# One core, macaron block in split fp32: turning two token units behind the first half of the first product

## What is computed

```python
x = x + 0.5 * ffn(layernorm(x))      # ffn: (silu(x @ Wg.T) * (x @ Wu.T)) @ Wd.T, hidden 2048
x = x + attn(layernorm(x))           # z = x @ W.T, four gated scans over time, layernorm, gamma, beta
x = x + 0.5 * ffn(layernorm(x))
```

## Time and profile before

| what | value |
|---|---|
| median of 3 runs | 1022.0 us (1021.89 to 1022.03) |
| the profiled execution, its own time | 1021.91 us |
| its span | 1020.1 us |
| TensorE matmul busy | 1014.9 us, 99% |
| VectorE, ScalarE, GpSimd busy | 671.1, 406.4, 162.1 us |
| granted TensorE clock, mean | 1.000 |

### The profile page before, as it was taken

The page is one execution under the profiler, slowest core; times in us unless marked ns, Lnnn a source line. Parts: engine busy times, 40 slices in busy tenths (PEclk is TensorE's granted clock), DMA queues, the critical chain, the costliest instruction groups (busy, mean ns, idle before and its releaser), DMA issues.

```text
span 1020.1 us, 12555 instructions
## 1 busy us (share of the span) xinstructions
PE 1014.9 (99%) x4512; PEld 841.5 (82%) x4512; DVE 671.1 (66%) x1013; ACT 406.4 (40%) x667; POOL 162.1 (16%) x187
## 2 busy tenths in 40 slices
PE   9999999999999999999999999999999999999998
PEld 8888888888888888888888888888888888888887
DVE  7755665598988687857978878786685333333342
ACT  6644445465433622224732363231382322222311
POOL 4123343125300200210430020021040000000000
PEclk9999999999999999999999999999999999999999
DMA  6688877778667555647856764454677565655255
GB/s 206 229 321 320 302 265 253 247 231 275 237 227 232 181 189 159 199 144 237 272 167 229 234 218 150 146 186 143 226 251 226 206 191 193 204 196 189 88 191 182
DMA packets 61710, 217.89 MB, mean 214 GB/s; under 512 B 6352, under 2 KB 15568, under 8 KB 53968
## 3 DMA queue, kind: packets, MB, share of 16 engines
q1 hardware_dynamic: 61072, 216.03, 63.1%
q10 hardware_dynamic: 576, 1.05, 0.3%
HBM read 170.92 MB, written 46.14 MB: 213 GB/s over the span
## 4 chain that ended last, share of the span: by engine, by line
PE 99%; DVE 1%; DMA 0%; DVEq 0%; issue 0%
PE ps_a L1538 8%; PE ps_a L1540 8%; PE ps_a L1539 8%; PE ps_b L1538 8%; PE ps_b L1540 8%; PE ps_b L1539 8%; PE ps_c L1538 7%; PE ps_c L1540 7%; PE ps_c L1539 7%; PE ps_d L1538 7%; PE ps_d L1540 7%; PE ps_d L1539 7%; PE aux L1539 3%; PE aux L1538 3%; PE aux L1540 3%; PE ps_d L1700 1%
## 5 line engine op out<-in xcount | busy, mean ns | idle before, releaser
L1035 DVE TENSOR_TENSOR tmp<-tmp,ps_c 128x512 f32<-128x512 f32 x59 | 40.4, 685 | 139.5 <-PE ps_c L1540 139.5
L1538 PE MATMUL ps_a<-xt,gu 128*128 128x512 f32 x304 | 118.3, 389 | 0.0
L1540 PE MATMUL ps_a<-xt,gu 128*128 128x512 f32 x304 | 118.3, 389 | 0.0
L1539 PE MATMUL ps_a<-xt,gu 128*128 128x512 f32 x304 | 118.3, 389 | 0.0
L1539 PE MATMUL ps_b<-xt,gu 128*128 128x512 f32 x286 | 111.3, 389 | 0.0
L1540 PE MATMUL ps_b<-xt,gu 128*128 128x512 f32 x286 | 111.3, 389 | 0.0
L1538 PE MATMUL ps_b<-xt,gu 128*128 128x512 f32 x286 | 111.3, 389 | 0.0
L1540 PE MATMUL ps_d<-dn,hid 128*128 128x512 f32 x256 | 99.6, 389 | 0.0
L1538 PE MATMUL ps_d<-dn,hid 128*128 128x512 f32 x256 | 99.6, 389 | 0.0
L1539 PE MATMUL ps_d<-dn,hid 128*128 128x512 f32 x256 | 99.6, 389 | 0.0
L1540 PE MATMUL ps_c<-xt,gu 128*128 128x512 f32 x236 | 91.8, 389 | 0.0
(11 more groups left out here) (204 smaller groups left out, 2111.5 us busy)
## 6 DMA issues: line engine op xcount, KB each, us to landing
dn<-dn_kept SPq DMA_DIRECT2D x112, 512.0 KB, 3.7
gu<-gu_kept SPq DMA_DIRECT2D x46, 1024.0 KB, 5.0
gu<-gu_kept SPq DMA_DIRECT2D x46, 768.0 KB, 5.6
gu_kept<-gu SPq DMA_DIRECT2D x14, 1024.0 KB, 4.3
gu_kept<-gu SPq DMA_DIRECT2D x14, 768.0 KB, 4.2
dn_kept<-dn SPq DMA_DIRECT2D x16, 512.0 KB, 5.1
h_t<-w_ffn_in SPq DMA_DIRECT2D x18, 256.0 KB, 4.8
x_tok<-w_ffn_in SPq DMA_DIRECT2D x18, 256.0 KB, 5.1
```

Source lines behind the costliest of these rows:

```text
L1035: dve.tensor_tensor(dst, u3s(si), p5_bank(si)[:, :], ALU.add).then_inc(c22_done, 1)
L1538: pe.matmul(dst, a_hi, b_hi, start=start, stop=False, skip_group_check=chained)
L1539: pe.matmul(dst, a_hi, b_lo, start=False, stop=False, skip_group_check=chained)
L1540: return pe.matmul(dst, a_lo, b_hi, start=False, stop=stop, skip_group_check=chained)
```

## The change

TensorE turns units 0 and 1 before the first product, as before. Units 2 and 3 are turned inside the first product, behind the first eight matmuls of the half that needs units 0 and 1 alone (high by high, low weights by high x). The filling matmuls stay behind unit 1. Nothing else is edited; the other engines' orders are the same.

```diff
@@ plain_first @@
                     if h == 0:
                         pe.wait_ge(raw_lo, 1)
                     plain_part(ps_a, 0, 0, 0, 1, 0, c)
+                    if h == 0:
+                        turn_x(2)
+                        turn_x(3)
                 for h, c in enumerate(halves):
                     pe.wait_ge(first_lo, 2 * h + 2)
@@ order of TensorE @@
             keep_warm(WARM)
-            for r in range(4):
+            for r in range(2):
                 turn_x(r)
```

## The result

| kernel | median, us | runs | ratio to before, 95% interval |
|---|---|---|---|
| before | 1022.00 (1021.85 to 1022.35) | 22 | |
| changed | 1023.53 (1023.33 to 1023.86) | 22 | 1.0015 [1.0009, 1.0021] |

The changed kernel is 1.5 us slower. By the bound of 0.2% that the prediction sets, this is no change; but the two sets of times don't overlap and the interval leaves out 1.

What follows compares the result with a forecast made beforehand. TensorE, busy 99% of the span, was taken to bound the kernel. Two waits of 0.50 and 0.97 us, 1.47 us in all, added to the profiled 1021.91 gave 1023.4 us; the range was 1022.7 to 1024.4 us.

Steps and rivals of the forecast that it cites:

- the bound of 0.2%: Whole kernel: about 0.2%, 2 us here, is what a measurement can tell from no change.
- The bound: Whole kernel: TensorE, busy 99%, has no slack behind the front, so its loss there arrives at the end nearly whole.
- First wait: Before the first half product: TensorE waits from 9.78 for ScalarE's conversion of unit 1, pace counting from 10.28; 0.50 us idle.
- the hop: From a ScalarE release to full TensorE pace: 0.14 us taken, bounds 0.03 and 0.17 us.
- Second wait: Before the first product's second half: TensorE waits for ScalarE's conversions of units 2 and 3 until 13.09; 0.97 us idle.
- What is late next: Behind the two conversions: ScalarE late by 1.47 us, VectorE by some 0.85, later waits costed at nothing; margins 1.5 us and more.
- the fourth rival: At 17.75 or a later conversion: a second engine's lateness, ScalarE's, holds TensorE; 1024.4 us, chance 0.04.
- Give-back: Behind the front up to the end: between 0 and 0.3 us of the delay might be recovered; taken as 0.
- The sum: Front of the kernel: idle times of 0.50 and 0.97 us make 1.47 us, carried to the end.
- The second rival: At about 12 to 13 us: the clock falls in the thin stretch, steps double, 2.3 us lost; 1025.7 us, chance 0.08.
- The third rival: At 13.09: the half ahead hides the conversions, or the delay is given back; 1022.4 or 1021.6 us, chance 0.08.

Runs made afterwards that it cites:

- The kernel with eight matmuls as cover: Against the changed kernel, units 2 and 3 turned behind the first four matmuls, eight more matmuls before the second half; 1022.65 us, +0.49 to before.
- the run with fifteen calls: Kernel before with 15 instead of 18 warming calls (30 instead of 36 matmuls); 1021.89 us, -0.04 to before.

## Why the prediction was right

**The bound.** As predicted: behind the front TensorE has no slack, and what it lost arrived whole. Between the two profiles the shift is 1.69 us at the second product (13.56 to 15.25), 1.68 at the start of the long stage (34.51 to 36.19) and 1.72 at the last matmul (1016.53 to 1018.25); of each, 0.14 is the late front of this execution. Each experiment's shift in the front and its time agree within 0.1 us (table).

**First wait.** Forecast 0.50 us, from 9.78 to a pace counted from 10.28; measured 0.59. Unit 1's conversion sets it, as said: the cover by unit 2's transposes took all but 0.12 us of it away. The kernel with eight matmuls as cover has this wait alone and lost 0.49 us by the medians, 0.59 in its trace. In the profile of the changed kernel unit 1's conversion is over at 9.21 + 1.07 = 10.28, the half product's first start is at 10.43, and counted back from the transposes its pace starts at 11.46 - 0.97 = 10.49. So the hop by the pace was 0.21 us, where I took 0.14 and gave 0.17 as the upper bound. The bound was too narrow, which is worth 0.07 us; the other 0.02 of this wait is that TensorE was free 0.12 us later than in the old profile, and the conversions stood 0.14 later.

**Second wait.** Forecast 0.97 us; measured, TensorE is free at 12.33 and starts at 13.23, and by the pace (16 matmuls, 1.94 us, ahead of 15.25) the restart counts from 13.31: 0.98 us. The conversion ended at 13.17, so this hop was 0.14 us, as taken. The reason, transposes then two conversions with nothing to do meanwhile, is shown from both sides: work put in there for nothing changes no time, and needed work put there takes off its own length (0.51 and 0.53 us by the medians for 0.48 us each).

**What is late next.** Costed at nothing, and nothing was found: no further wait of TensorE appears, so the fourth rival did not happen. ScalarE's next conversion of weights is at 13.06, 11.37 before; less the 0.14 of this profile, it is late by 1.55 (forecast 1.47). The end of VectorE's low parts is at 12.72 + 1.29 = 14.01, and was at 12.23 + 0.68 = 12.91: late by 0.96 after the same 0.14 is taken off, still less than TensorE. The forecast had 0.85: it let unit 3's low part start behind unit 3's conversion, at about 13.1, but VectorE has unit 2's low part to end first.

**Give-back.** Taken as 0 of 0 to 0.3 us. Nothing came back: the shift is no smaller at 36.19 and at 1018.25 than at 15.25.

**The sum.** 1.47 forecast, 1.53 by the medians and 1.55 in the profile. Of the profile's 0.08 us over the forecast, 0.07 is the hop of the first restart and 0.01 the second wait. The forecast time of 1023.4 starts from the one profiled execution, 1021.91; from the median of 1022.00 the same sum gives 1023.47, against 1023.53.

**The clock.** The second rival did not happen: no step doubled, and the clock was 1.00 from 10.43 to 13.23. The Trainium skill ("TensorE: Matmul & The Clock Gate", "Part 4: PE-mode transpose") says that transposes don't count as activity in the way of matmuls. By that rule only eight matmuls spoke for the full clock in that stretch, and it stayed up. The kernel before without filling matmuls shows a stronger case. Its last warming matmul starts at 7.44, then TensorE idles and makes nothing but transposes until the half product at 10.46, whose matmuls have the usual steps of 0.12 us:

```profile
8.46 2.25 PE L1748 MATMUL ps_d<-ident,hid 128*128 128x128 f32 x16 [0.74 <-DVE hid L1156]
```

Whether the transposes kept the clock up, or it would have stayed up without them, no run here shows; so nothing here speaks clearly for or against the page.

**The other side.** The third rival needed the conversions to be hidden. They are hidden in the kernel before, by having the transposes ahead; moving them behind eight matmuls put the first half early and the end late. Even there the cover is only just long enough:

```profile
11.60 0.81 PE L1700 MATMUL ps_a<-xt,gu 128*128 128x256 f32 x5
```

The second half starts at 11.60, 0.11 us behind the end of unit 3's conversion (10.89 + 0.60 = 11.49), and its first step, in the single records, is 0.17 us in place of 0.12. With no slack in the old cover, every matmul taken out of it can show as lost time, which fits the even trade of the experiments.

## What to carry to other kernels

Where TensorE turns data that another engine must convert before TensorE can use it, the transposes are the head of a chain: they go first, and the independent matmuls go behind them as cover. In this kernel putting matmuls ahead gained nothing, since the first half's result isn't used by itself. The loss was the time from the last transpose to the restart of TensorE (0.98 us, with ScalarE's conversions in it) less the work left in between, and on top of it the first conversion's wait that the moved transposes had covered. Since the engine that bounds this kernel has no slack, a loss of 1.5 us in the first 15 us reappeared whole after 1000 us, and can be read in the front of a profile far better than in the total time.

## What was not expected

The moment at which TensorE's steps go from the 1.2 to the 2.4 GHz level differs between executions of the same first instructions. These are the warming matmuls of the changed kernel, grouped from 1.5 to 7.4 us (count, busy us, mean ns):

```profile
L1691 PE MATMUL ps_b<-ident 128*128 128x128 f32 x27 | 6.1, 427 | 1.6 <-POOL ident L982 1.6
```

and those of the kernel with unit 3 alone moved, from 4.9 to 7.2 us:

```profile
L1691 PE MATMUL ps_b<-ident 128*128 128x128 f32 x22 | 2.6, 275 | 0.0
```

In the first the long steps last until about 7.7 us, in the second they are over at 4.7; in the earlier trace rows it was about 6. When the change comes late, 36 warming matmuls end behind the moment when the first normalized unit is ready, and the front starts late: 8.58 in the changed kernel's profile instead of 8.38. That may be part of the spread of a few tenths between executions (not shown: the run with fifteen calls could not tell), and it is one reason why two profiles should be laid over each other at the first common event and not at the start of the span. In the profile where it came early, TensorE idled for 1.50 us ahead of its first transpose, and the transposes behind it still ran at their usual pace:

```profile
8.77 1.12 PE L1750 MATMUL ps_d<-ident,hid 128*128 128x128 f32 x8 [1.50 <-DVE hid L1156]
```

The first transpose stands later still here, at 8.77 against 8.38 in the earlier trace rows, and not because of the warming matmuls: TensorE waited for VectorE's first normalized unit. So the front moved between these profiles for at least two reasons.
